# Two gathered 64x64 products with residuals: transposes in TensorE's idle stretch, own PSUM banks for the second block, and a later release of the x loads

## The reference

```python
w = weights[subjects]                       # weights: (8, 64, 64), subjects: (128,)
x = x + jnp.einsum('bct,bcd->bdt', x, w)
w = weights[conditions]                     # weights: (200, 64, 64), conditions: (128,)
x = x + jnp.einsum('bct,bcd->bdt', x, w)    # x: (128, 64, 512) float32, 16.8 MB in, 16.8 MB out
```

## Time and profile before

| what | value |
|---|---|
| runs | 93.46, 93.66, 95.83 us, median 93.66 us |
| the profiled execution's own time | 94.32 us |
| its span, first to last instruction | 92.5 us |
| mean granted TensorE clock | 0.988 |
| TensorE matmul busy | 72.8 us, 79% of the span |
| VectorE, ScalarE, GpSimd busy | 60.9, 50.6, 23.8 us |
| DMA | 35.92 MB, mean 388 GB/s |

### The profile page before, as it was taken

How to read it: one execution, slowest core, us unless ns; L and a number is a source line. 1 busy time by engine, 2 the same in 40 slices (tenths; PEclk the granted TensorE clock), 3 DMA queues, 4 the chain that set the end, 5 groups by cost and what they waited for, 6 DMA issues and landing times.

```text
span 92.5 us, 2284 instructions
## 1 busy us (share of the span) xinstructions
PE 72.8 (79%) x836; PEld 38.7 (42%) x836; DVE 60.9 (66%) x115; ACT 50.6 (55%) x95; POOL 23.8 (26%) x124
## 2 busy tenths in 40 slices
PE   0400009999299999999999999999999999999700
PEld 0200008899154545435445544754444444444200
DVE  0086003389527887888778788878788788787740
ACT  2300001468626776777567677677576676676630
POOL 4220009989999989000000000000000000000000
PEclk9999999999999999999999999999999999999995
DMA  0999999999999999999999999999999999879695
GB/s 16 330 457 390 430 395 420 413 411 405 416 405 404 400 411 404 409 407 416 398 411 413 418 409 418 420 409 420 420 421 418 414 418 416 361 310 388 276 402 228
DMA packets 9180, 35.92 MB, mean 388 GB/s; under 512 B 721, under 2 KB 850, under 8 KB 9042
## 3 DMA queue, kind: packets, MB, share of 16 engines
q1 hardware_dynamic: 8880, 33.56, 90.4%
q0 software_dynamic: 144, 2.10, 5.4%
q10 hardware_dynamic: 146, 0.13, 0.5%
HBM read 19.01 MB, written 16.78 MB: 387 GB/s over the span
## 4 chain that ended last, share of the span: by engine, by line
PE 73%; DMA 13%; DVE 6%; issue 2%; DVEq 1%; ACT 1%; POOLq 0%; ACTq 0%
PE psum L225 61%; DMA w_rows<-in_L_cond_weights_dram,cond 10%; PE psum L206 7%; PE psum L187 6%; DVE w L244 5%; DMA cond<-in_itok_B_dram 3%; DVEq L64 1%; DVE xy L266 1%; ACT m_diag L258 1%; DVE w_rows L306 0%; POOLq L160 0%; ACTq L250 0%; POOLq L151 0%
## 5 line engine op out<-in xcount | busy, mean ns | idle before, releaser
L225 PE MATMUL psum<-xy,m_diag 64*128 64x512 f32 x256 | 56.6, 594 | 0.0
L266 DVE COPY xy<-psum 64x512 f32<-64x512 f32 x64 | 43.7, 684 | 12.7 <-PE psum L225 11.7
L266 ACT COPY xy<-psum 64x512 f32<-64x512 f32 x64 | 37.2, 581 | 19.1 <-PE psum L225 18.3
L225 PEld LDWEIGHTS psum<-xy,m_diag 64*128 64x128 f32 x256 | 24.4, 187 | 27.7 <-issue 27.1
L168 POOL COPY w0b<-w0t 64x64 f32 x112 | 21.6, 235 | 10.3 <-DMA w_rows<-in_L_cond_weights_dram,cond 8.5
L187 PE MATMUL psum<-ident,w_rows 128*64 128x128 f32 x64 | 9.5, 323 | 9.3 <-DVE w_rows L306 9.3
L244 ACT COPY w<-psum 64x256 f32<-64x256 f32 x16 | 5.8, 364 | 15.3 <-PE psum L187 14.5
L187 PEld LDWEIGHTS psum<-ident,w_rows 128*64 128x64 f32 x64 | 8.4, 158 | 10.7 <-DVE w_rows L306 9.8
L244 DVE COPY w<-psum 64x256 f32<-64x256 f32 x16 | 6.7, 417 | 3.4 <-PE psum L187 3.0
L206 PE MATMUL psum<-w,w0b 64*32 64x64 f32 x512 | 6.5, 224 | 1.8 <-ACT m_diag L258 0.9
L258 DVE TENSOR_SCALAR m_diag<-psum,mask 128x256 f32<-128x256 f32 (+2 forms) x14 | 6.7, 517 | 1.9 <-PE psum L206 1.7
(11 more groups left out here) (6 smaller groups left out, 0.8 us busy)
## 6 DMA issues: line engine op xcount, KB each, us to landing
xy<-in_x_dram SPq DMA_DIRECT2D x15, 1024.0 KB, 19.5
out_dram<-xy SPq DMA_DIRECT2D x15, 1024.0 KB, 11.1
xy<-in_x_dram SPq DMA_DIRECT2D x2, 512.0 KB, 7.4
out_dram<-xy SPq DMA_DIRECT2D x2, 512.0 KB, 3.4
w_rows<-in_L_cond_weights_dram ACTq DMA_DIRECT2D x1, 128.0 KB, 2.6
cond<-in_itok_B_dram SPq DMA_DIRECT2D x1, 0.5 KB, 2.4
subjects<-in_itok_B_dram ACTq DMA_DIRECT2D x1, 0.5 KB
w_rows<-in_L_cond_weights_dram,cond POOLq DMA_INDIRECT x1, 9.5
```

The costliest lines, as they stand in the source:

```text
L225: last = nc.tensor.matmul(psum[:, 2 * (s % Y_RING) + h, :], m_diag[rows, odd, v % M_RING, j, :], xy[rows, s, j * T:(j + 1) * T], start=j = ...
L266: copy(xy[rows, s, i * T:(i + 1) * T], psum[HALVES[i], 2 * (s % Y_RING) + h, :]).then_inc(done, 1)
```

## The change

`WARM = 52` transposes of `w0_rows` are added on TensorE directly behind the four that are needed; their output goes to the six banks of the W1 ring and nobody reads it. The M of the second block goes to banks 4 and 5 (`M_BANKS`), and `products(1)` no longer waits for the copies of the first M. SyncE loads slots 2 and 3 as one unit right behind the first unit, and then waits until VectorE has made its 16 copies of W0 (`s_w0b_early`) before the other fourteen units; it waited for the gather to be sent, ahead of slot 3. The mask is written by eight small memsets on VectorE instead of five on GpSimd.

```diff
-    M_BANK = 6
+    M_BANKS = [6, 4, 6, 6, 6, 6, 6]
+    WARM = 52
...
             load(0, 2)
-            load(2, 1)
-
-            sp.wait_ge(s_gather_sent, 1)
-            load(3, 1)
+            load(2, 2)
+
+            sp.wait_ge(s_w0b_early, EARLY * UNIT)
             for v in range(2, UNITS):
                 load(2 * v, 2)
...
-            nc.gpsimd.memset(mask[:, :], 0.0).then_inc(s_zeros, 1)
-            pool.wait_ge(s_zeros, 2)
-            for r, rows in enumerate(QUARTERS):
-                nc.gpsimd.memset(mask[rows, r % 2:r % 2 + 1], 1.0).then_inc(s_mask, 1)
-            pool.wait_ge(s_mask, SLOT)
...
             last.then_inc(s_w0_turned, 1)
+            for n in range(WARM):
+                nc.tensor.transpose(psum[0:C, n % W1_RING, 0:P], w0_rows[:, n % ROWS, :], ident[:, :])
...
-                if k >= 1:
+                if k >= 2:
+
                     pe.wait_ge(s_m_v, 2 * k)
                     pe.wait_ge(s_m_s, 2 * k)
...
-                                last = nc.tensor.matmul(psum[QUARTERS[r], M_BANK + odd, at:at + C],
+                                last = nc.tensor.matmul(psum[QUARTERS[r], M_BANKS[k] + odd, at:at + C],
...
-                    pe.wait_ge(s_x[v], 32 if v == 1 else 16)
+                    pe.wait_ge(s_x[v], 16)
...
-                      psum[:, M_BANK + odd, at:at + n * J * C].rearrange("q (w e i) -> q w i e", i=J, e=Q),
+                      psum[:, M_BANKS[k] + odd, at:at + n * J * C].rearrange("q (w e i) -> q w i e", i=J, e=Q),
...
-            eng.wait_ge(s_mask, SLOT)
+            eng.wait_ge(s_mask, 2 * SLOT)
...
         @block.vector
         def _(dve):
+            for r, rows in enumerate(QUARTERS):
+                for b in range(2):
+                    nc.vector.memset(mask[rows, b:b + 1], 1.0 if b == r % 2 else 0.0).then_inc(s_mask, 1)
```

More of the change, by code:

```diff
@@ L89, in bass_cond_residual_kernel @@
         s_gather = sem("s_gather")
-        s_gather_sent = sem("s_gather_sent")
         s_mask = sem("s_mask")
@@ L154, in _ @@
                 in_=w1_dram.rearrange("s d e -> s (d e)"),
-                in_offset=bass.IndirectOffsetOnAxis(ap=cond[:, 0:1], axis=0),
-                engine_sem=s_gather_sent).then_inc(s_gather, 16)
+                in_offset=bass.IndirectOffsetOnAxis(ap=cond[:, 0:1], axis=0)).then_inc(s_gather, 16)
             pool.wait_ge(s_subjects, 16)
```

## The result

The changed kernel took 97.66 us (median of 4 runs, 97.26 to 97.83), the kernel before 93.8 us: 1.042 times as long, 95% interval 1.036 to 1.047. I had forecast 92.7. The profiled executions differ by 97.26 - 94.32 = 2.9 us, the spans by 95.4 - 92.5; the one of before lay half a microsecond above its median, the one of after is the fastest of its four. Medians here are of all executions, while ratios leave out those that took over 1.5% more than the fastest of the same kernel.

A forecast was written before the change was run, and what follows sets the result against it. TensorE and the DMA queue were taken to bound the kernel within a few microseconds of each other. TensorE's terms, -2.3 - 0.46 + 0.3, gave -2.5 us; the queue let 1.0 through: 93.66 - 1.0 = 92.7 us, range 91.1 to 93.9.

The forecast's parts named there:

- the price of the 52 transposes: Added TensorE work before W1: it ends at 12.3 us, hidden ahead of W1's start at 14.2, and raises the clock.
- The gather: Load of W1, sharing the DMA queue with slot 3: lands 0.3 us later, at 13.9 us.
- nothing is saved: Mask memsets moved to VectorE: they had ended at 2.13 us, the gather was sent at 4.10; cost 0.
- The clock at T0: T0, TensorE's start on W1, at 14.2 us: clock still high, as the 1.9 us gap is under the recorded 2.8.
- The term of 2.3 us: W1 stage at the high clock: products 8.0 us after T0 instead of 10.37, a gain of 2.3 us.
- Own banks for the second M: Products(1) runs during the copies of the first M, so application 0 starts 0.46 us earlier.
- The queue's floor: Last stores: the DMA queue's slowest engine lands the last unit at 91.1 us at the earliest, letting only 1.0 us through.
- Rivals: Four: TensorE leads (0.20, 91.2 us), transposes in the way (0.07, 94.7), clock low (0.08, 93.5), queue starved (0.05, 93.7).

The follow-up runs named there:

- e5: The kernel before with 26 small float32 matmuls (104 instructions) added behind the W0 transposes; 97.67 us, ratio 1.040.
- e8: The changed kernel with the load order of before and 14 long matmuls (56 instructions) instead of the 52 transposes; 98.60 us, ratio 1.049.
- e1: The changed kernel without its 52 added transposes; 94.76 us, ratio 1.006.
- e9: The changed kernel with its two last blocks of four units split into four blocks of two; 95.31 us, ratio 1.012.
- e15: The kernel before with the mask written on VectorE and nothing else changed; 94.60 us, ratio 1.003.
- e6: The kernel before with the 52 transposes and nothing else of the change; 95.48 to 99.13 us.
- e10: The changed kernel with blocks of two units, the load order of before and 64 transposes instead of 52; 93.07 us, ratio 0.989.
- e16: The same kernel as e14, run once more for another profile; the traced execution took 95.19 us.
- e14: The kernel before with own banks for the second M, 62 transposes and blocks of two units; 93.13 us, ratio 0.988.
- e4: The changed kernel with the load order of before; 97.48 us.
- e13: The changed kernel with blocks of two units and the mask memsets back on GpSimd; 93.95 us, ratio 0.988, in two pairs.
- e11: The changed kernel without transposes and with the load order of before; 94.59 us, ratio 1.006.
- e12: The kernel before with blocks of two units; 94.08 to 96.94 us.

## Why the prediction was wrong, point by point

- **The step that failed is the price of the 52 transposes.** I priced them by TensorE's time and the clock, found both hidden or good, and left out that they are 104 instructions in a program whose instructions come to TensorE piece by piece: that cost stood in the sum as nothing. Measured: 1.14 + 1.50 = 2.64 us of the 2.84. I had TensorE end 2.5 us earlier and it ended 2.84 later; of these 5.3 us the stalls are 2.6, the missing gain in W1 1.7 and the gather 0.9. Shown by e5 (the same number of other instructions, the same stalls), e8 (48 fewer, the long gap 48 further on), e1 (none, none) and e9 (shorter bursts, none). No rival of mine had this mechanism. "Runtime: NRT & Kernel Launch" of the Trainium skill, in its section on instruction fetch, has the 16 KiB blocks of 256 instructions, and the trace agrees with both (packets of 16 KB, 256 instructions from gap to gap). It calls the cost of crossing a boundary mostly hidden; by the count above, five of the changed kernel's seven crossings show no gap, but the two others cost 0.86 and 1.24 us, and one in e8 1.97.
- **The gather: 0.3 us later as I put it, 1.2 in fact.** The direction was right, by a sum of bytes; the early sending, which I took for harmless ("nothing is saved"), goes with a landing as much later as the held loads do. I had taken the gather as sent at 4.10 still; without the memsets on GpSimd it went at 3.40 (e15, with nothing else changed, at 3.42), though they had ended at 2.13; why they held it up is open.
- **The clock at T0.** The clock rose on transposes alone (24 of 52 at the low rate, 22 forecast), against the rule of "TensorE: Matmul & The Clock Gate", Part 4, of the Trainium skill that the prediction cites. That the count came so close was luck: the rise stood at 9.4 us here, at 6.6 in e6 and at 6.2 in e10, with the same transposes. The clock also fell again, and this I had ruled out from the length of the gap (1.9 us forecast, 2.5 in fact). The length does not settle it: after 3.15 us in e16 and 1.91 in e10 the clock stayed high, after 2.13 to 2.58 in e14, e9, e4, e13, e8, the changed kernel and e6 it fell. The term of 2.3 us was right in e10 (10.37 to 8.11), and 0.59 here. Even the 0.59 need not be the transposes': without any of them the stage took 9.40 to 9.97 us in e15, e11, e1 and e12, so the 10.37 that I started from was the longest of its kind, and 8.11 is 1.3 to 2.3 us less.
- **Own banks for the second M: 0.46 forecast, 0.50 measured.** Right.
- **The queue's floor.** In the changed kernel TensorE led to the end. In e10 TensorE ended 1.5 us earlier than before and the last store landed at 90.8 against 92.1, 1.3 us earlier: the queue held back 0.2. The landing is the one that I forecast within 0.3 us (91.1), but TensorE's path alone would have given 90.6, so e10 does not prove the floor. e14 and the quicker pair of e13, with other starts, come to the same 93.1 us, which fits it; no trace shows where TensorE ended in those executions, so the floor stays open.
- **Rivals.** None gave over 94.7. The slower side needed a wait of TensorE far from the place of the edit, 40 us behind it, and none of them had one.

## What to carry to other kernels

Count added instructions as instructions, not only by their time, even in idle stretches at the start: in a long unrolled program they shift where every later 16 KB piece ends, and where the end falls near the end of a burst that runs through most of a piece in some 1.4 us, TensorE may stand still for the next one. Idle time put down to "issue" inside a burst, with an instruction packet in the DMA view ahead of it, is its mark; what helped here was shorter bursts between long instructions, and other numbers of added instructions moved or removed the gaps. A transfer that is sent earlier need not land earlier: look at its landing, and at what else the earlier sending releases.

## What I had not expected of the hardware

- 128 transposes of 64 by 64, back to back for 13.8 us, left TensorE's clock low (0.108 us each to the last, and the W1 transposes behind them at 418 ns), where 52 of 128 by 128 had raised it 2.4 to 5.2 us after their start (e6, the changed kernel).
- A gather sent 0.7 us earlier landed 0.7 us later (e15 against the kernel before, 14.26 and 13.58 us, the same loads but slot 3 issued 0.6 us sooner), and its first packet started at 6.7 us in both.
- A stall of 1.97 us in an otherwise busy TensorE was followed by 3.4 us at half clock (e8), so that a stall can cost about twice itself.
